# Attention scores in pairs of heads with one maximum and one exponential each, and a new table of beats for a four-layer kernel

## The chip, the cores and the metric

The kernel runs on one core of a Trainium2 chip. The metric is the time of one execution on the device, in microseconds (us); three runs of the kernel before gave 785.09, 787.24 and 787.25, median 787.24. The core has five engines that work side by side: TensorE (PE in the profile, with its weight loads as PEld), VectorE (DVE), ScalarE (ACT), GpSimd (POOL) and SyncE (SP, which here only issues transfers). They agree through semaphores alone.

## The reference

The input x has 8 images of 128 channels and 16 x 16 positions. Four layers follow each other; all arrays are float32.

```
x = gamma * (softmax(b @ c) @ d) + x        # L0: b, c (16 rows) and d (128 rows) are 1x1 convolutions of x
x = x + proj(attn(qkv(groupnorm(x))))       # L1: 8 heads of 16, all 256 positions of an image
t = tokens(x)                               # 256 tokens of 128 for each image
y = layernorm(t); t = t + softmax(y @ y.T) @ y                      # L2: self-attention without weights
y = layernorm(t); p = top-2 gate weights of softmax(y @ Wg)
t = t + sum over i in 0,1 and e in 0..7 of gelu((y * p_i) @ W1[e] + b1[e]) @ W2[e]    # d 128, dff 512, + b2
h = layernorm(t); q, k = rope(rmsnorm(h @ Wq)), rope(rmsnorm(h @ Wk))
t = t + softmax(q @ k.T / 4, keys s-31..s) @ v @ Wo                 # L3: 8 heads of 16, window of 32 tokens
h = layernorm(t); t = t + shared(h) + sum over the top 2 of 8 experts of p_e * (silu(h Wg_e) * (h Wu_e)) Wd_e
```

The dense experts of L2 run all 8 experts for both gate weights: 32 pieces of 128 hidden rows for each group of 512 tokens, 128 pieces in all.

## The kernel before, in words

**Tiling.** Work goes by groups of two images (512 tokens, 4 groups) and, in attention, by images. Attention is done sixteen times: images 0 to 7 in layer L1, then 8 to 15, which are the same images in layer L3. An attention is done in two halves of four heads each.

**Order.** Every engine runs the same outer loop over beats `s` (0 to LAST - 1, 224 of them) and issues, in a fixed order inside the beat, its share of whatever part stands in that beat. A beat is no length of time: a beat in which an engine has nothing to issue costs it nothing. Tables at lines 52 to 65 say in which beat a part stands: L0_AT (layer L0 of a group), P1_AT (norm and projection of L1), ATT_AT (an attention), TAIL_AT (output projection), L2_AT (self-attention and gates of L2), SPREAD_AT, FF_AT (first piece of the dense experts), END_AT, PREP_AT (norm, projection and rope of L3), ROUTER_AT and EXPERT_AT (the last mixture of experts). From beat FF_AT = 36 on, 128 beats hold one piece ("turn") of the dense experts each.

**One attention.** For image a, counted from its beat in ATT_AT: beats 0 and 2, scores of a half (`scores`, L399, queries in rows) and their row maxima on VectorE (`highest`, L1015); beats 1 and 3, the shifts so found are added to the queries' spare row (`add_shift`) after TensorE has turned them (`turn_shifts`, L413); beats 4 and 6, scores again with keys in rows (`scores_turned`, L431) and their exponentials on ScalarE (`exps`, L750, to ET); beats 5 and 7, the product with the values (`values`, L454); beat 8, the result is turned (`turn_o`, L467). In L1 two images stand four beats apart or less, so that parts of two halves alternate. In L3 a half's scores are 320 columns for a head in place of 512, and a product with a band constant puts the window's mask into the bank first (L391).

**Banks.** PSUM has 8 banks of 128 x 512. Bank 0 takes the up products of the dense experts, bank 2 their down products, banks 3 to 6 (QUAD_BANK) one half's scores, a bank for a head, and 1 and 7 (MISC) all else in turn. Each bank has a semaphore for filled and one for emptied; `take` waits until a bank is empty before TensorE writes. The last experts take gate, up and weight products into banks 0 and 3, 4 and 6, and 5.

**Dense experts.** A turn: up product into bank 0 (`ff_up`, two matmuls of 512 columns, L540), VectorE multiplies it by the two gate weights into z_s, 1024 wide (`ff_gate`, L1090, which empties the bank), ScalarE adds the bias and takes gelu (L809), GpSimd adds the two gated halves (`hidden`, L1278), TensorE multiplies down (`ff_down`, L547). Gelu and exponential need different function tables on ScalarE, so the gelus of eight turns are issued together.

**GpSimd** takes the normalisations between layers: `norm` first works out the roots (`newton`, L1264), then four products of 128 x 128 (L1271); also the group norm of L1 (L1258). Two sets of constants for the later layers are made in beats: `prepare_late` on GpSimd in beat 18, the rotary tables on VectorE (`tables`) in beat 34.

## Time and profile before

| what | value |
|---|---|
| median of three runs | 787.24 us |
| the profiled execution | 783.05 us |
| its span, from first to last instruction | 781.3 us |
| granted TensorE clock, mean over the span | 0.884 of full speed |
| TensorE busy | 633.1 us, 81% of the span |
| VectorE, ScalarE, GpSimd busy | 390.9, 343.4, 333.7 us |
| instructions | 9513 |
| chain that ended last | TensorE 51%, VectorE 16%, GpSimd 14%, issue 10%, ScalarE 8% |
| VectorE's gates (L1090) | 128, mean 1222 ns |
| row maxima (L1015) | 128, mean 583 ns |
| exponentials (L750) | 128, mean 522 ns, with 10 table loads of 1283 ns |

The profile is one execution recorded on the chip. "Busy" is the time in which an engine had an instruction under way. The chain that ended last is followed back from the last instruction, at each step to what released it, and its shares say on which engine the span was spent. The granted clock is the share of full speed that TensorE was allowed; it has two levels, 1.2 and 2.4 GHz, and a value between them is a mean over a stretch. A timeline lists instructions in order of their start; in brackets stands how long the engine had been idle before, and whose end released it.

### The profile page before, as it was taken

To read this page: it belongs to the slowest core of one execution; us is meant where nothing else is said; L and a number is where in the kernel's file an instruction comes from. 1 tells how busy PE (TensorE), PEld (TensorE's weight loads), DVE (VectorE), ACT (ScalarE), POOL (GpSimd) and SP (SyncE) were. 2 spreads that over 40 slices of the span, in tenths; PEclk is the share of its full clock that TensorE was granted. 3 is DMA by queue.
4 is the path that set the end of the run, shared out by engine and by line. 5 is a ranking of instruction groups with operands and counts; after the bars stand their busy time and mean duration, and the time that the engine had idled before them with its cause. 6 is when DMAs were issued, how large, how long until landed. Compare 5 with 4: busy or idle time off the path is not lost.

```text
span 781.3 us, 9513 instructions
## 1 busy us (share of the span) xinstructions
PE 633.1 (81%) x3266; PEld 324.7 (42%) x3266; DVE 390.9 (50%) x799; ACT 343.4 (44%) x544; POOL 333.7 (43%) x620
## 2 busy tenths in 40 slices
PE   7788988677888977887997869996689889757768
PEld 5565455444344442434443424442334344334422
DVE  3464441557375564674556385644675434531233
ACT  2423224136466465365455346653744634212222
POOL 2543411606174186696146685428671534200300
PEclk9997566789999999988999889999999999855789
DMA  6600000000000000000000000000000000000000
GB/s 211 146 1 1 1 1 1 0 1 1 1 0 1 1 1 1 1 0 0 2 0 2 0 1 0 1 1 1 0 0 1 1 1 14 13 1 1 0 14 13
DMA packets 10226, 8.59 MB, mean 11 GB/s; under 512 B 4026, under 2 KB 8132, under 8 KB 10180
## 3 DMA queue, kind: packets, MB, share of 16 engines
q1 hardware_dynamic: 10180, 8.00, 3.6%
q8 instruction: 27, 0.44, 0.3%
q14 instruction: 19, 0.16, 0.1%
HBM read 6.94 MB, written 1.05 MB: 10 GB/s over the span
## 4 chain that ended last, share of the span: by engine, by line
PE 51%; DVE 16%; POOL 14%; issue 10%; ACT 8%; DMA 0%; POOLq 0%; SPq 0%; DVEq 0%; ACTq 0%
PE bank L540 9%; PE bank L547 8%; POOL h_s L1278 4%; ACT ET L750 4%; DVE shiftpad L1015 4%; DVE z_s L1090 3%; POOL xn_l L1271 3%; PE bank L266 3%; PE bank L399 3%; PE bank L431 3%; PE bank L454 2%; PE bank L413 2%; PE bank L591 2%; PE bank L576 2%; PE bank L391 1%
## 5 line engine op out<-in xcount | busy, mean ns | idle before, releaser
L1090 DVE TENSOR_TENSOR z_s<-bank,PB 128x1024 f32<-128x1024 f32 x128 | 156.4, 1222 | 164.7 <-PE bank L540 162.6
L1278 POOL TENSOR_TENSOR h_s<-z_s 128x512 f32<-128x512 f32 x128 | 163.0, 1299 | 153.7 <-ACT z_s L809 135.4
L540 PE MATMUL bank<-XN_C,W 128*128 128x512 f32 x256 | 144.1, 646 | 34.3 <-DVE z_s L1090 33.7
L547 PE MATMUL bank<-h_s,W 128*128 128x512 f32 x256 | 145.3, 651 | 1.4 <-ACT y_s L816 1.0
L809 ACT ACTIVATE z_s<-z_s,b 128x1024 f32<-128x1024 f32 x128 | 137.2, 1141 | 11.0 <-DVE z_s L1090 10.8
L1015 DVE TENSOR_REDUCE shiftpad<-bank 128x2 f32<-128x512 f32 (+1 forms) x128 | 66.6, 583 | 53.9 <-PE bank L399 29.4
L540 PEld LDWEIGHTS bank<-XN_C,W 128*128 128x128 f32 x256 | 44.7, 199 | 101.8 <-DVE z_s L1090 79.3
L750 ACT ACTIVATE ET<-bank 128x512 f32<-128x512 f32 (+1 forms) x128 | 55.8, 522 | 57.0 <-PE bank L431 30.1
L1264 POOL TENSOR_SCALAR root_l<-mv_l 128x4 f32<-128x4 f32 x12 | 2.8, 232 | 168.8 <-DVE mv_l L1046 168.3
L547 PEld LDWEIGHTS bank<-h_s,W 128*128 128x128 f32 x256 | 44.5, 202 | 37.0 <-issue 31.4
L771 ACT COPY XN_C<-bank 128x512 f32<-128x512 f32 x16 | 9.4, 585 | 68.2 <-PE bank L266 68.1
L758 ACT COPY o_raw<-bank 128x256 f32<-128x256 f32 x32 | 11.9, 373 | 61.9 <-PE bank L454 37.5
L1271 POOL TENSOR_SCALAR xn_l<-R,mv_l,root_l 128x128 f32<-128x128 f32 x48 | 37.7, 800 | 1.3
L399 PE MATMUL bank<-K,Q 16*128 16x256 f32 x256 | 33.1, 514 | 3.8 <-ACT ET L750 3.8
L750 ACT ACT_TABLE_LOAD x10 | 12.8, 1283 | 51.8 <-PE bank L435 39.1
L1141 DVE TENSOR_TENSOR z_s<-z_s,bank 128x512 f32<-128x512 f32 (+1 forms) x20 | 13.7, 684 | 35.8 <-PE bank L579 27.6
L413 PE MATMUL bank<-ident,shiftpad 128*128 128x128 f32 x64 | 15.8, 336 | 18.6 <-DVE shiftpad L1015 17.0
L454 PE MATMUL bank<-ET,V 128*17 128x256 f32 x256 | 22.9, 488 | 7.3 <-ACT ET L750 5.2
L399 PEld LDWEIGHTS bank<-K,Q 16*128 16x128 f32 x256 | 21.7, 231 | 12.2 <-ACT ET L750 7.8
L266 PE MATMUL bank<-ident,xn_l 128*128 128x128 f32 x48 | 9.7, 336 | 18.4 <-POOL xn_l L1271 18.4
L413 PEld LDWEIGHTS bank<-ident,shiftpad 128*128 128x128 f32 x64 | 8.1, 166 | 38.7 <-issue 38.7
L840 ACT ACTIVATE z_s<-bank 128x512 f32<-128x512 f32 (+1 forms) x20 | 12.0, 602 | 25.8 <-PE bank L576 25.7
(246 smaller groups left out, 961.3 us busy)
## 6 DMA issues: line engine op xcount, KB each, us to landing
W<-in_L_ffn_W_dram SPq DMA_DIRECT2D x1, 2048.0 KB, 8.7
XN_C<-in_x_dram SPq DMA_DIRECT2D x4, 256.0 KB, 3.0
out_dram<-z_s SPq DMA_DIRECT2D x4, 256.0 KB, 2.2
Wgate<-in_L_ffn_W_gate_dram SPq DMA_DIRECT2D x1, 256.0 KB, 4.2
Wup<-in_L_ffn_W_up_dram SPq DMA_DIRECT2D x1, 256.0 KB, 4.8
Wdown<-in_L_ffn_W_down_dram SPq DMA_DIRECT2D x1, 256.0 KB, 4.3
early<-in_L_conv_W_qkv_dram SPq DMA_DIRECT2D x1, 192.0 KB
early<-in_L_conv_Wd_dram SPq DMA_DIRECT2D x1, 64.0 KB, 1.9
```

Of the source, the lines that this page charges most:

```text
L266: ins = nc.tensor.transpose(to[:, t * P:(t + 1) * P], source(t), ident[:, :])
L399: ins = nc.tensor.matmul(to[j][:, t * N:(t + 1) * N], q[:, t * P:(t + 1) * P], k, start=True, stop=True)
L413: ins = nc.tensor.transpose(to[:, t * P:(t + 1) * P], shiftpad[:, i % 2, t, :, :].rearrange("p j r -> p (j r)"), ident[:, :])
L454: ins = nc.tensor.matmul(to, v, E[:, kt * N:(kt + 1) * N], start=(kt == 0), stop=(kt == NT - 1), skip_group_check=True)
L540: nc.tensor.matmul(to[:, :], W1[:, f // 4, f % 4 * P:(f % 4 + 1) * P], XN_C[:, pair(g)], start=True, stop=True).then_inc(filled("u", t)[0], 1)
L547: ins = nc.tensor.matmul(bank[D_BANK][:, :], W2[:, f, :], h_s[:, t % H_RING, :], start=(f == 0), stop=(f == FT - 1)).then_inc(s_dn, 1)
L750: nc.scalar.activation(ET[:, i % 2 * SLOTS + j, 0:width(a)], content("T", (i, j))[:, 0:width(a)], ACT.Exp).then_inc(emptied("T", (i, j))[0 ...
L809: nc.scalar.activation(z, z, ACT.Gelu, bias=b1[:, f:f + 1]).then_inc(s_g, 1)
L1015: nc.vector.tensor_reduce(shiftpad[:, i % 2, :, j, HD], content("S", (i, j))[:, 0:width(a)].rearrange("p (t k) -> p t k", t=NT), AX.X, ALU ...
L1090: nc.vector.tensor_tensor(z_s[:, t % Z_RING, :].rearrange("p (w n) -> p w n", w=2), content("u", t)[:, None, :].broadcast_to([P, 2, W]), P ...
L1271: ins = nc.gpsimd.tensor_scalar(xn[n][:, c, :], R[:, tile(g, c)], mv[n][:, g, c, 0:1], y[:, c:c + 1], ALU.subtract, ALU.mult)
L1278: nc.gpsimd.tensor_tensor(h_s[:, t % H_RING, :], z_s[:, t % Z_RING, 0:W], z_s[:, t % Z_RING, W:2 * W], ALU.add).then_inc(s_h, 1)
```

## The change

Four things are changed together.

1. Banks 3 to 6 become one tensor `quad`. Scores and turned scores fill all four banks in their step and report each pair of heads with one semaphore (`KEEPER`, `fill`, `take_two`); `highest` and `exps` take two heads in one instruction (1024 columns in L1, 640 in L3). There are 64 of each in place of 128.
2. The steps of an attention are set by a table, `STEPS`. SLOW (images whose beat lies among the turns) puts shifts two beats behind scores, values two behind the turned scores, and the end in beat 9. FAST (images before the turns, and those behind beat 160) puts them in successive beats: scores 0 and 1, shifts and turned scores 1 and 2, values 2 and 3, end 4.
3. The beats are laid out anew. Turns begin at beat 32 and the last beat is 203. Layer L0 of groups 2 and 3 stands in beats 10 and 16, among the first attentions; all four projections of L1, layer L2 of group 0 and most of that of group 1 stand ahead of the first turn. The constants of `prepare_late` and `tables` move behind the first turn. In a beat, TensorE now issues shifts, values, turned scores and scores in this order.
4. The last experts take other banks: those of group 3 use banks 0 and 3, 1 and 5, and 7, the others bank 0 and the ring. Group 2's pass stands in the beats of the last attention, whose exponentials and sigmoid products use different tables on ScalarE.

The core of the diff:

```diff
-FF_AT = 36
+FF_AT = 32
 GELU_AT, DOWN_LAG = 5, 7
 Z_RING, H_RING = 8, 6
-L0_AT = (0, 3, 6, 9)
-P1_AT = (8, 12, 30, 44)
-ATT_AT = (9, 13, 17, 21, 33, 41, 49, 57, 89, 97, 121, 129, 153, 161, 185, 189)
-TAIL_AT = (22, 30, 50, 66, 106, 138, 170, 198)
-L2_AT = (27, 37, 61, 77)
-SPREAD_AT = (35, 45, 69, 101)
+L0_AT = (0, 3, 10, 16)
+P1_AT = (7, 13, 22, 28)
+ATT_AT = (8, 10, 14, 16, 37, 45, 53, 61, 93, 101, 117, 125, 149, 157, 179, 181)
+TAIL_AT = (15, 21, 56, 72, 112, 136, 168, 186)
+L2_AT = (20, 26, 61, 77)
+SPREAD_AT = (30, 40, 72, 104)
 END_AT = tuple(FF_AT + FT * (g + 1) + DOWN_LAG for g in range(GROUPS))
-PREP_AT = tuple(FF_AT + FT * g + 45 for g in range(3)) + (177,)
-ROUTER_AT = (113, 145, 177, 205)
-EXPERT_AT = (172, 178, 200, 211)
-LAST = 224
-
-U_BANK, D_BANK, QUAD_BANK, MISC = (0,), 2, 3, (1, 7)
-XG_BANK, XU_BANK, XW_BANK = (0, 3), (4, 6), 5
+PREP_AT = (81, 109, 141, 172)
+ROUTER_AT = (118, 141, 173, 191)
+EXPERT_AT = (168, 174, 180, 196)
+LAST = 203
+U_BANK, D_BANK, QUAD_BANK, MISC, MISC_FIRST = 0, 2, 3, (1, 7), (1, 7, 0)
+KEEPER = (0, 1, 2, 3, 3, 5, 5, 7)
+SLOW = {"S": (0, 2), "MT": (2, 4), "T": (4, 6), "PV": (6, 8), "OT": 9, "later": 0}
+FAST = {"S": (0, 1), "MT": (1, 2), "T": (1, 2), "PV": (2, 3), "OT": 4, "later": 0}
+STEPS = [FAST if at < FF_AT or at > FF_AT + TURNS else SLOW for at in ATT_AT]
...
+            def fill(what, i, banks):
+                kept = KEEPER[banks[0]]
+                was = max(content_of[b] for b in banks)
+                if was:
+                    pe.wait_ge(bank_emptied[kept], was)
+                fills[kept] += 1
+                for b in banks:
+                    content_of[b] = fills[kept]
+                turn_of[what, i] = banks[0], fills[kept]
+                return bank[banks[0]]
             def take(what, i, b=None):
-
                 if b is None:
-                    b = MISC[turns[0] % len(MISC)]
-                    turns[0] += 1
-                if fills[b]:
-                    pe.wait_ge(bank_emptied[b], fills[b])
-                fills[b] += 1
-                turn_of[what, i] = b, fills[b]
-                return bank[b]
+                    ring = MISC if beat[0] >= FF_AT else MISC_FIRST
+                    turns[ring] += 1
+                    b = ring[turns[ring] % len(ring)]
+                return fill(what, i, (b,))
+            def take_two(what, i, jj):
+                return fill(what, i, (QUAD_BANK + 2 * jj, QUAD_BANK + 2 * jj + 1))
...
-                to = [take("S", (i, j), QUAD_BANK + j) for j in range(SLOTS)] if a >= IMAGES else [None] * SLOTS
+                for jj in range(2):
+                    take_two("S", (i, jj), jj)
...
-                        if t == NT - 1:
-                            ins.then_inc(filled("S", (i, j))[0], 1)
+                        if t == NT - 1 and j % 2 == 1:
+                            ins.then_inc(filled("S", (i, j // 2))[0], 1)
...
-            def exps(a, half):
+            def exps(a, half, jj):
                 i = a * 2 + half
-                if i >= 2:
+                if i >= 2 and jj == 0:
                     act.wait_ge(*filled("pv", i - 2))
-                for j in range(SLOTS):
-                    act.wait_ge(*filled("T", (i, j)))
-                    nc.scalar.activation(ET[:, i % 2 * SLOTS + j, 0:width(a)], content("T", (i, j))[:, 0:width(a)], ACT.Exp).then_inc(
-                        emptied("T", (i, j))[0], 1)
+                at = i % 2 * SLOTS + 2 * jj
+                act.wait_ge(*filled("T", (i, jj)))
+                nc.scalar.activation(ET[:, at:at + 2, 0:width(a)], quad[:, 2 * jj:2 * jj + 2, 0:width(a)], ACT.Exp).then_inc(emptied("T", (i, jj))[0], 1)
...
-            def highest(a, half):
+            def highest(a, half, jj):
                 i = a * 2 + half
-                if i >= 2:
-                    dve.wait_ge(*filled("MT", i - 2))
-                elif i == 0:
-                    dve.wait_ge(s_pads, 5)
-                for j in range(SLOTS):
-                    dve.wait_ge(*filled("S", (i, j)))
-                    nc.vector.tensor_reduce(shiftpad[:, i % 2, :, j, HD], content("S", (i, j))[:, 0:width(a)].rearrange("p (t k) -> p t k", t=NT),
-                                            AX.X, ALU.max, negate=True).then_inc(emptied("S", (i, j))[0], 1)
+                if jj == 0:
+                    if i >= 2:
+                        dve.wait_ge(*filled("MT", i - 2))
+                    elif i == 0:
+                        dve.wait_ge(s_pads, 5)
+                at = slice(2 * jj, 2 * jj + 2)
+                dve.wait_ge(*filled("S", (i, jj)))
+                nc.vector.tensor_reduce(shiftpad[:, i % 2, :, at, HD].rearrange("p t j -> p j t"),
+                                        quad[:, at, 0:width(a)].rearrange("p j (t k) -> p j t k", t=NT),
+                                        AX.X, ALU.max, negate=True).then_inc(emptied("S", (i, jj))[0], 1)
...
-                    to = take("xg", (g, k), XG_BANK[k % 2])
+                    to = take("xg", (g, k), (0, QUAD_BANK)[k % 2 if g == GROUPS - 1 else 0])
...
-                    to = take("xu", (g, k), XU_BANK[k % 2])
+                    to = take("xu", (g, k), (1, 5)[k % 2] if g == GROUPS - 1 else None)
...
-                        to = take("xw", (g, k), XW_BANK)
+                        to = take("xw", (g, k), 7 if g == GROUPS - 1 else None)
...
-                if s == 34:
+                if s == FF_AT:
...
-                if s == 18:
+                if s == FF_AT + 10:
```

Loops that named beats by `k in (0, 2)` and the like now compare with STEPS in the same way on all engines; lines below L262 move down by some 20 to 28.

What stands in TensorE's row one step before the turns, in the attention of images 2 and 3: before,

```order
L399 MATMUL bank<-K,Q 128x256 x8
L454 MATMUL bank<-ET,V 17x256 x8
L413 MATMUL bank<-ident,shiftpad 128x128 x2
L431 MATMUL bank<-Q,K 128x256 x8
L399 MATMUL bank<-K,Q 128x256 x8
L454 MATMUL bank<-ET,V 17x256 x8
L413 MATMUL bank<-ident,shiftpad 128x128 x2
L467 MATMUL bank<-ident,o_raw 128x128 x4
L431 MATMUL bank<-Q,K 128x256 x8
L399 MATMUL bank<-K,Q 128x256 x8
```

and now:

```order
L420 MATMUL quad<-K,Q 128x256 x8
L320 MATMUL bank<-XN_C,Wbc 128x512
L287 MATMUL bank<-ident,XN_C 128x128 x4
L326 MATMUL bank<-WdT,XN_C 128x128 x4
L434 MATMUL bank<-ident,shiftpad 128x128 x2
L475 MATMUL bank<-ET,V 17x256 x8
L452 MATMUL quad<-Q,K 128x256 x8
L502 MATMUL bank<-Wp,oT 128x128 x4
L420 MATMUL quad<-K,Q 128x256 x8
```

L399 (now L420) are scores, L431 (L452) turned scores, L454 (L475) values, L413 (L434) shifts, L467 and L502 parts of the output. Before, one kind of product follows another of the other half and the values stand two rows behind the scores; now layer L0 of another group stands between scores and shifts, and values and turned scores follow the shifts directly.

In TensorE's row ahead of the first up product (L540, now L561): before,

```order
L481 MATMUL bank<-Wp,oT 128x128 x4
L266 MATMUL bank<-ident,xn_l 128x128 x4
L399 MATMUL bank<-K,Q 128x256 x8
L527 MATMUL bank<-Wg,XN_C 128x8 x4
L266 MATMUL bank<-ident,xn_l 128x128 x4
L413 MATMUL bank<-ident,shiftpad 128x128 x2
L399 MATMUL bank<-K,Q 128x256 x8
L266 MATMUL bank<-ident,gate 128x128 x8
L540 MATMUL bank<-XN_C,W 128x512
```

and now:

```order
L537 MATMUL bank<-xn_l,early 128x128 x8
L287 MATMUL bank<-ident,xn_l 128x128 x8
L548 MATMUL bank<-Wg,XN_C 128x8 x4
L518 MATMUL bank<-XN_C 128x256 x4
L527 MATMUL bank<-ident,early 128x128 x8
L376 MATMUL quad<-XN_C,Wqk 128x512 x4
L379 MATMUL bank<-WvT,XN_C 128x128 x4
L537 MATMUL bank<-xn_l,early 128x128 x8
L287 MATMUL bank<-ident,gate 128x128 x8
L287 MATMUL bank<-ident,xn_l 128x128 x4
L561 MATMUL bank<-XN_C,W 128x512
```

Here L266 (L287) turns a normalised or gate tile, L527 and L548 `Wg` are gate logits, L516 (L537) with `early` is the self-attention of L2, L376 and L379 a projection of L1. The projection of group 3 and all of group 1's layer L2 up to the turning of its normalised tokens (`xn_l` x4) now stand ahead of the first up product, where scores of two images stood.

In ScalarE's row at the last attention (ET is the exponential, o_raw a copy of the values' product): before,

```order
L750 ACT_TABLE_LOAD
L750 ACTIVATE ET<-bank 128x320 x4
L758 COPY o_raw<-bank 128x256
L750 ACTIVATE ET<-bank 128x320 x4
L758 COPY o_raw<-bank 128x256
L750 ACTIVATE ET<-bank 128x320 x4
L758 COPY o_raw<-bank 128x256
L750 ACTIVATE ET<-bank 128x320 x4
L758 COPY o_raw<-bank 128x256
```

and now:

```order
L776 ACT_TABLE_LOAD
L776 ACTIVATE ET<-quad 128x2x320 x2
L865 ACT_TABLE_LOAD
L865 ACTIVATE z_s<-bank 128x512
L783 COPY o_raw<-bank 128x256
L776 ACT_TABLE_LOAD
L776 ACTIVATE ET<-quad 128x2x320 x2
L865 ACT_TABLE_LOAD
L865 ACTIVATE z_s<-bank 128x512
L783 COPY o_raw<-bank 128x256
```

The activation of an expert block (z_s, L865) now stands between the exponentials of two halves, and a table load ahead of each; ACT has 42 table loads in all, 36 before.

## Rows read from the trace of the kernel before

**Rows 1.** Windows: us, busy (instructions) of each engine, PEclk, DMA share, GB/s.

```profile
66.00:131.00 65.00, 56.47 (x370) 33.73 (x370) 23.25 (x52) 20.98 (x45) 20.27 (x57) 0.61 0.00 1
78.30:89.30 11.00, 10.01 (x71) 4.82 (x70) 5.77 (x11) 2.44 (x5) 8.79 (x22) 0.66 0.00 0
161.60:612.00 450.40, 374.66 (x1859) 177.88 (x1858) 261.94 (x441) 247.20 (x346) 243.64 (x373) 0.95 0.00 1
682.80:731.00 48.20, 31.49 (x253) 19.63 (x254) 9.80 (x24) 9.06 (x22) 0.00 (x0) 0.50 0.00 1
```

**Rows 2.** Timeline to the first up product: start, us, instruction, idle before and releaser.

```profile
138.78 0.24 POOL L1264 TENSOR_SCALAR root_l<-mv_l 128x4 f32<-128x4 f32 x1 [17.89 <-DVE mv_l L1046]
...
142.79 3.14 POOL L1271 TENSOR_SCALAR xn_l<-R,mv_l,root_l 128x128 f32<-128x128 f32 x4
...
161.64 1.91 PE L540 MATMUL bank<-XN_C,W 128*128 128x512 f32 x2
```

**Rows 3.** Timeline of VectorE: gates.

```profile
163.69 1.23 DVE L1090 TENSOR_TENSOR z_s<-bank,PB 128x1024 f32<-128x1024 f32 x1 [3.87 <-PE bank L540]
...
228.50 1.21 DVE L1090 TENSOR_TENSOR z_s<-bank,PB 128x1024 f32<-128x1024 f32 x1
...
302.69 1.23 DVE L1090 TENSOR_TENSOR z_s<-bank,PB 128x1024 f32<-128x1024 f32 x1 [1.29 <-PE bank L540]
...
483.12 1.22 DVE L1090 TENSOR_TENSOR z_s<-bank,PB 128x1024 f32<-128x1024 f32 x1 [0.25 <-PE bank L540]
...
507.62 1.22 DVE L1090 TENSOR_TENSOR z_s<-bank,PB 128x1024 f32<-128x1024 f32 x1 [0.28 <-PE bank L540]
...
612.26 1.23 DVE L1090 TENSOR_TENSOR z_s<-bank,PB 128x1024 f32<-128x1024 f32 x1 [0.96 <-PE bank L540]
```

**Rows 4.** Timeline of one step of the attention before the experts.

```profile
83.27 2.06 ACT L750 ACTIVATE ET<-bank 128x512 f32<-128x512 f32 x4 [2.27 <-PE bank L431]
84.01 3.45 PE L399 MATMUL bank<-K,Q 16*128 16x256 f32 x16 [0.82 <-ACT ET L750]
...
86.73 2.48 DVE L1015 TENSOR_REDUCE shiftpad<-bank 128x2 f32<-128x512 f32 x4 [3.86 <-PE bank L399]
87.39 1.91 PE L454 MATMUL bank<-ET,V 128*17 128x256 f32 x16
...
90.06 2.09 PE L431 MATMUL bank<-Q,K 17*128 17x256 f32 x16
...
92.88 3.53 PE L399 MATMUL bank<-K,Q 16*128 16x256 f32 x16 [0.73 <-ACT ET L750]
```

**Rows 5.** Timeline: first projection and scores, and the last values before the experts.

```profile
28.62 2.45 POOL L1258 TENSOR_SCALAR XN_C<-XN_C,gm,root 128x256 f32<-128x256 f32 x2
...
36.69 3.60 PE L355 MATMUL bank<-XN_C,Wqk 128*128 128x512 f32 x8
...
45.76 1.15 PE L399 MATMUL bank<-K,Q 16*128 16x256 f32 x16
...
131.17 1.06 PE L454 MATMUL bank<-ET,V 128*17 128x256 f32 x16 [0.81 <-ACT early L783]
```

**Rows 6.** Timeline of TensorE behind the dense experts.

```profile
672.62 1.97 PE L576 MATMUL bank<-XN_C,Sgate 128*64 128x512 f32 x2
...
676.99 1.91 PE L266 MATMUL bank<-ident,early 128*128 128x128 f32 x16
...
682.87 1.23 PE L391 MATMUL bank<-bandb,identb 128*128 128x320 bf16 x4 [2.92 <-ACT K L742]
...
751.17 1.06 PE L561 MATMUL bank<-router,XN_C 128*128 128x8 f32 x8
```

**Rows 7.** Timeline of ScalarE: table load and exponentials of the last attention.

```profile
695.84 1.28 ACT L750 ACT_TABLE_LOAD   x1 [13.31 <-PE bank L435]
697.14 1.43 ACT L750 ACTIVATE ET<-bank 128x320 f32<-128x320 f32 x4
```

More of the change, by code:

```diff
@@ L441, in values @@
                 i = a * 2 + half
-                for j in range(SLOTS):
-                    pe.wait_ge(*emptied("T", (i, j)))
+                for jj in range(2):
+                    pe.wait_ge(*emptied("T", (i, jj)))
                 if half == 0:
@@ L598, in _ @@
             for s in range(LAST):
+                beat[0] = s
                 for g in range(GROUPS):
@@ L618, in _ @@
                 for a in range(2 * IMAGES):
-                    k = s - ATT_AT[a]
-                    if k in (0, 2):
-                        scores(a, k // 2)
-                    if k in (1, 3):
-                        turn_shifts(a, k // 2)
+                    for half in range(2):
+                        if s == ATT_AT[a] + STEPS[a]["S"][half]:
+                            scores(a, half)
                 if 0 <= s - FF_AT - DOWN_LAG < TURNS:
```

99 lines of the change are left out of this document (54 added, 45 removed).

## The prediction

> **What bounds the kernel now.** I read the windows by stage first. In the long middle stage, the 128 turns of the dense experts, TensorE is busy 374.66 of 450.4 us at a clock of 0.95, and no other engine passes 262 [rows 1]. In the attention of the last two images, 48.2 us, TensorE is busy 31.49 us and the clock is 0.50, the lower of its two levels (1.2 of 2.4 GHz). In the attention before the experts, 66 to 131 us, it is 0.61, although TensorE is busy 56.47 of 65. So there are three stages with three limits: a chain of dependent steps at a low clock, a stage nearly full of matmuls, and a chain again. The first up product stands at 161.64 [rows 2], which makes stage A; its gates run from 163.69 to 612.26 [rows 3], stage B; the rest to 781.3 is C.
>
> Second, the timeline of one step of A. From scores to scores it is 92.88 - 84.01 = 8.87 us [rows 4]; TensorE idles only 0.73 to 0.82 in it, on the exponentials. The maxima (2.48) and exponentials (2.06) of one half lie beside the products of another image's half. Scores or turned scores take 2.09 at the low level; at the high one 1.15 [rows 5].
>
> Third, the gates of B. Alone, a turn lasts 1.29 + 1.23 = 2.52 us: gate, next up product into the one bank, gate. An image of layer 3 with its eight beats takes 507.62 - 483.12 = 24.50 [rows 3], not far above 8 x 2.52 = 20.2.
>
> **Merged instructions.** Two heads' maxima are now one instruction of 1024 columns. VectorE's gate of 1024 took 1.23 [rows 3], four maxima of 512 take 2.48 [rows 4], so two wide ones cost 2.46 by the gate, at best 2.2 if half of the fixed part falls away, at worst 2.5. ScalarE's four exponentials take 2.06; two wide ones I bound by 1.9 and 2.3 in the same way and take 2.1. The merge itself is worth nothing I can see; what it changes is grain. Scores now wait for both exponentials before their first product, where before the banks came free one at a time.
>
> **Stage A.** (1) The start gets earlier. Group 0 is normalised on POOL at 28.62 + 2.45 = 31.07, yet its projection stood at 36.69, behind products of group 2 [rows 5]. Now it follows group 1 directly: 31.1 + 3.6 for the projection + 1.2 for what stands between = scores at 35.9, against 45.76. (2) The steps get longer. Before the experts, transposed shifts, turned scores, and the scores of the next half stand in one beat, so a half's whole path lies in line: maximum 2.0 to 2.1 behind the scores, shifts 0.4 (0.7 at the low level), values of the half before 1.0 (1.91), which hide the addition of the shift, turned scores 1.15 (2.09), exponentials less the part beside the products 1.75 (1.6), scores 1.15 (2.09). That is 7.5 at the high level and 10.4 at the low. Seven steps are 53 or 73. The last half's rest to its values adds 9.3 or 12. Group 1's projection and the parts of groups 2 and 3 that stick out of the waits add 9 or 12. The eighth values end at 35.9 + 71.3 = 107 or 133; before, 131.17 + 1.06 = 132.2 [rows 5]. (3) More stands between them and the first up product: two groups' layer 2, two projections. POOL normalises three things in a row, and one such took 138.78 to 145.93, 7.15 [rows 2]. From the eighth values: 5 until POOL has its first, 3 x 7.15 for three, 13 for gate logits, scores, turning, projection and output of group 1's layer 2, then 10.5 for its statistics (2.5), POOL again (7.15) and its turning, which stands ahead of the first up product in TensorE's row: 50, and 58 at the low level. Before, it was 29.4. First up product: 157 or 191. With nearly half of the way at each level I take 174: A = +12, between -4 and +29.
>
> At this place a row and a rule meet. The row: the clock was 0.50 where TensorE waited a third of the time, but 0.61 also where it waited little [rows 1]. The Trainium skill (TensorE: Matmul & The Clock Gate, "A second HAM failure mode: psum-queue depth-cycling") says that a TensorE which idles briefly between groups of matmuls while banks go round swings between its two levels and loses throughput. The trace agrees, and shows the low level with little idling too. By that rule alone A would be +29; by the full level it would be -4.
>
> **Stage B.** Before, 448.6 us. The first sixteen turns took 228.50 - 163.69 = 64.8 [rows 3], since group 1's layer 2, group 3's projection and an image stood in them. Those two now lie in A. What is left: five turns alone, 5 x 2.52 = 12.6; three beats with scores, where a gate stands behind two wide maxima, 3.5 each, 10.5; eight beats of an image of layer 1, at 3.15 each a little above the 24.50 / 8 = 3.06 of layer 3, 25.2: 48.3, so -16.5. Images of layer 3: the beats with two kinds of products get longer (values 0.6 into the beat of turned scores), the emptied ones fall no lower than 2.52; 24.5 +- 1 against 24.50, nothing. The stalls on maxima and exponentials in the other images of layer 1 go, by my estimate 1.5 each for three: -4.5. What is late next there is the gate. Other tails, routers and projections trade collisions on POOL, 0 +- 6. B = -21, between -6 and -28. POOL's late constants, 22 instructions over 11.0 us [rows 1], move into the tenth turn; POOL's idle half of B covers them, and without that cover they cost up to 11. The rotary tables move to turn 0 and hold one gate for about 1 us, which I leave in the rounding.
>
> **Stage C.** The turning of the last queries (676.99) stood behind the fourth block of an expert pass, which begins at 672.62 [rows 6]; it is now before it, but ScalarE takes that block's activation ahead of the copies. Scores start 5.9 us after the turning now, 6.1 then: -4. Ahead of that, POOL does the experts' norm before the attention's and TensorE waits less for maxima and exponentials: -4, bounds 0 and -11. Then four steps in line, with the third group's expert blocks in them, which before followed until the router at 751.17, 68.3 after the first scores. Each step has two switches of ScalarE's table. In line: gate product 1.0, load 1.3, activation 0.6, two products on VectorE 1.4, shift 0.4, turned scores 1.6, load 1.3, two exponentials of 640 columns 1.4, scores 1.7, and 0.4 of signals: 11.1. First scores to second 11, three steps and the rest of the fourth 29, then values, last blocks, output projection and norm 24.5: 64.5 at the high level, some 13 more at the low one. In between, 71: +3. The last pass is as long as before. C = -5, between -12 and +2.
>
> The row on loads: the load starts at 695.84, the first exponential at 697.14, so 1.30 each [rows 7]. The Trainium skill (ScalarE: Activation LUTs, "Table sets: the hidden batching unit") advises against this change: do all calls of one table set together; and its section "What ACT_TABLE_LOAD costs" gives some 2.66 us a switch with draining. The trace shows no such drain. By the page the six more switches would cost an estimated 8 us more and the sum below would rise by that.
>
> **Sum.** 783.05 + 12 - 21 - 5 = 769 for the profiled execution (span 781.3 and 1.75 around it). The median of the runs, 787.24, is 4.2 above that execution; carried over, 773.
>
> **Rivals.** First, slower: the clock stays low through both chains. Place: the half's path in line in A and C; price: 17 us in A and 7 in C on top of the forecast, that is A +29, B -21, C +2, 793, with the 4.2 797. For it: 0.50 and 0.61 [rows 1]. Against: layer 0 and expert products of 128 rows now stand in the steps. It decides from the point where about four fifths of both chains are at the low level: A + C run from -16 to +31, and at +21 the gain of B is eaten. Second, the high level nearly throughout: A -4, C -12, B -21: 746, so 750. For it the same products; against it the waits of 2 us in each step. Third, the change doesn't do in B what it says: the gate's round trip of 2.52 fills every emptied beat, and the first sixteen turns save only 10 and the layer 3 images cost 1 each for four: B = -6, sum 784, so 788, no change or a little slower. For it [rows 3]; against it only that the moved products surely leave.
>
> **Chances.** Forecast 0.48, low clock 0.20, high clock 0.20, beats bound 0.12. The forecast's own range is 760 to 786. The range to 8 in 10 goes from 749 to 798, which takes in the ends of A and C. About 0.3%, 2.4 us, is what a measurement tells from no change. Faster: 0.48 less 0.02, 0.20, and 0.05 of the third, 0.71. Same: 0.02 and 0.04, 0.06. Slower: the first and the rest of the third, 0.23.
>
> **What would show it.** First scores near 36 and eighth values between 107 and 133, with the clock of that stretch beside; the first up product between 157 and 191, waiting for POOL's norm; sixteen turns in about 48; an image of layer 3 in 24 to 25.5; wide maxima of 1.2 and wide exponentials near 1.05; a step of the last attention near 11 with loads of 1.3. I am wrong if the first up product comes before 150, if an image of layer 3 falls under 23, or if a wide instruction takes twice the time of two narrow ones.

## The result, and the profile after

The changed kernel takes 806.28 us (median of four runs, 805.22 to 807.16) beside 786.32 for the kernel before: ratio 1.0254, 95% interval 1.0231 to 1.0277, slower. 773 was forecast, with 798 as the upper end. The profiled execution took 805.89, its span is 804.0; that is 22.7 more than before.

Cut at the gates into the prediction's stages, with the stage of the turns in two, from the timelines of VectorE (A ends with the first gate):

| kernel | A | first 16 turns | other turns | C | span |
|---|---|---|---|---|---|
| before | 163.7 | 64.8 | 383.8 | 169.0 | 781.3 |
| changed | 182.1 | 56.9 | 397.8 | 167.3 | 804.0 |
| difference | +18.4 | -7.9 | +14.0 | -1.7 | +22.7 |
| forecast | +12 | -16.5 | -4.5 | -5 | -14 |

The gates that make the cuts, from VectorE's timeline of the changed kernel (start, us, instruction, idle before); they answer to [rows 3]:

```profile
182.12 1.22 DVE L1118 TENSOR_TENSOR z_s<-bank,PB 128x1024 f32<-128x1024 f32 x1 [11.31 <-PE bank L561]
...
188.90 1.23 DVE L1118 TENSOR_TENSOR z_s<-bank,PB 128x1024 f32<-128x1024 f32 x1 [2.17 <-PE bank L561]
192.30 1.22 DVE L1118 TENSOR_TENSOR z_s<-bank,PB 128x1024 f32<-128x1024 f32 x1 [1.68 <-PE bank L561]
...
238.98 1.21 DVE L1118 TENSOR_TENSOR z_s<-bank,PB 128x1024 f32<-128x1024 f32 x1
...
636.73 1.22 DVE L1118 TENSOR_TENSOR z_s<-bank,PB 128x1024 f32<-128x1024 f32 x1 [0.67 <-PE bank L561]
```

A turn alone takes 192.30 - 188.90 = 3.40 here; in [rows 3] it took 2.52. The windows say why (us, busy and instructions of each engine, granted clock, DMA share, GB/s), as in [rows 1]:

```profile
36.20:126.00 89.80, 68.87 (x539) 43.92 (x540) 37.53 (x71) 27.91 (x49) 18.31 (x55) 0.75 0.00 1
126.00:179.90 53.90, 30.52 (x150) 22.82 (x150) 17.03 (x63) 13.92 (x34) 24.59 (x73) 0.78 0.00 0
179.90:213.00 33.10, 26.15 (x63) 10.64 (x64) 16.85 (x34) 8.32 (x8) 7.53 (x6) 0.50 0.00 0
182.10:636.70 454.60, 375.00 (x1836) 179.50 (x1837) 256.56 (x406) 237.74 (x293) 244.30 (x375) 0.92 0.00 1
```

The first row is the attention of images 0 to 3, the second what stands between its last values and the first up product: there TensorE is busy 30.5 of 53.9 us. The third row is the first turns, at 0.50, the low level.

TensorE's timeline of stage A, which answers to [rows 2] and [rows 5]:

```profile
36.22 1.15 PE L420 MATMUL quad<-K,Q 16*128 16x256 f32 x16
...
124.94 1.06 PE L475 MATMUL bank<-ET,V 128*17 128x256 f32 x16 [0.16 <-issue]
...
145.37 0.88 PE L287 MATMUL bank<-ident,xn_l 128*128 128x128 f32 x4 [3.40 <-POOL xn_l L1301]
152.56 1.11 PE L287 MATMUL bank<-ident,xn_l 128*128 128x128 f32 x4 [6.31 <-POOL xn_l L1301]
...
178.06 1.11 PE L287 MATMUL bank<-ident,xn_l 128*128 128x128 f32 x4 [8.85 <-POOL xn_l L1301]
179.94 2.05 PE L561 MATMUL bank<-XN_C,W 128*128 128x512 f32 x2 [0.77 <-ACT XN_C L796]
```

The eighth values end at 126.0, 6.2 earlier than before. From there to the first up product it is 53.9 us in place of 29.4, and 18.6 of them are three waits for GpSimd's norms.

Among the other turns the two longest are turn 108, 11.1 us from gate to gate, and turn 44, 10.0. GpSimd and TensorE around turn 44:

```profile
327.43 0.23 POOL L1294 TENSOR_SCALAR root_ff<-mv_ff 128x4 f32<-128x4 f32 x1 [1.02 <-DVE mv_ff L1074]
...
337.07 0.23 POOL L1294 TENSOR_SCALAR root_l<-mv_l 128x4 f32<-128x4 f32 x1
...
341.04 3.13 POOL L1301 TENSOR_SCALAR xn_l<-R,mv_l,root_l 128x128 f32<-128x128 f32 x4
```

```profile
336.80 1.12 PE L561 MATMUL bank<-XN_C,W 128*128 128x512 f32 x2
344.23 1.11 PE L287 MATMUL bank<-ident,xn_l 128*128 128x128 f32 x4 [6.30 <-POOL xn_l L1301]
345.14 1.92 PE L568 MATMUL bank<-h_s,W 128*128 128x512 f32 x2
```

The end of a group's experts (beat 71) and group 3's output projection (beat 72) each need a norm on GpSimd; they run one after the other, and TensorE stands in its row at the second one's turning (L287) for 6.3 us with every later turn behind it. Turn 108 is the same pair (beats 135 and 136), with a wait of 6.56:

```profile
570.44 1.11 PE L287 MATMUL bank<-ident,xn_l 128*128 128x128 f32 x4 [6.56 <-POOL xn_l L1301]
```

### The profile page after: what moved, and what is told of

Its sections match the earlier page's. It is cut to its first block, busy times and chain, and to the rows that moved or that the text cites. A ratio compares the mean times of both kernels' runs of the same rounds, so it can differ in the third digit from the quotient of the medians.

```text
span 804.0 us, 9310 instructions
## 1 busy us (share of the span) xinstructions
PE 631.7 (79%) x3266; PEld 325.0 (40%) x3266; DVE 383.5 (48%) x735; ACT 346.9 (43%) x486; POOL 333.1 (41%) x620
## 4 chain that ended last, share of the span: by engine, by line
PE 50%; DVE 17%; POOL 14%; issue 11%; ACT 6%; DMA 0%; POOLq 0%; DVEq 0%; SPq 0%; ACTq 0%
PE bank L561 10%; DVE z_s L1118 7%; PE bank L568 7%; POOL h_s L1308 5%; POOL xn_l L1301 3%; PE bank L597 3%; PE quad L420 2%; DVE shiftpad L1042 2%; PE quad L452 2%; ACT ET L776 2%; PE bank L287 2%; PE bank L612 2%; PE bank L475 2%; PE quad L376 2%; PE bank L600 1%
## 5 line engine op out<-in xcount | busy, mean ns | idle before, releaser
L561 PE MATMUL bank<-XN_C,W 128*128 128x512 f32 x256 | 151.0, 674 | 47.9 <-DVE z_s L1118 46.4
L568 PE MATMUL bank<-h_s,W 128*128 128x512 f32 x256 | 143.0, 644 | 7.3 <-POOL h_s L1308 7.3
L561 PEld LDWEIGHTS bank<-XN_C,W 128*128 128x128 f32 x256 | 46.1, 207 | 126.5 <-DVE z_s L1118 103.3
L1042 DVE TENSOR_REDUCE shiftpad<-quad 128x4 f32<-128x1024 f32 (+1 forms) x64 | 62.5, 1019 | 62.6 <-PE quad L420 33.9
L776 ACT ACTIVATE ET<-quad 128x1024 f32<-128x1024 f32 (+1 forms) x64 | 51.8, 861 | 30.3 <-PE quad L452 24.4
L568 PEld LDWEIGHTS bank<-h_s,W 128*128 128x128 f32 x256 | 45.2, 199 | 47.9 <-issue 33.9
L783 ACT COPY o_raw<-bank 128x256 f32<-128x256 f32 x32 | 11.9, 372 | 86.3 <-PE bank L479 43.7
L287 PE MATMUL bank<-ident,xn_l 128*128 128x128 f32 x48 | 10.8, 365 | 45.1 <-POOL xn_l L1301 45.1
L420 PE MATMUL quad<-K,Q 16*128 16x256 f32 x256 | 22.3, 470 | 11.0 <-ACT ET L776 10.8
L1277 POOL TENSOR_TENSOR R<-early,bp_all 128x512 f32<-128x512 f32 x4 | 5.1, 1267 | 61.3 <-DVE early L974 61.3
L287 PEld LDWEIGHTS bank<-ident,xn_l 128*128 128x128 f32 x48 | 6.9, 180 | 51.4 <-POOL xn_l L1301 50.9
L865 ACT ACTIVATE z_s<-bank 128x512 f32<-128x512 f32 (+1 forms) x18 | 10.7, 596 | 29.1 <-PE bank L597 29.1
L434 PE MATMUL bank<-ident,shiftpad 128*128 128x128 f32 x64 | 14.7, 317 | 10.9 <-issue 8.5
L452 PE MATMUL quad<-Q,K 17*128 17x256 f32 x256 | 21.2, 452 | 1.1 <-DVE Q L1050 1.0
```

Of the source, the lines that this page charges most:

```text
L287: ins = nc.tensor.transpose(to[:, t * P:(t + 1) * P], source(t), ident[:, :])
L420: ins = nc.tensor.matmul(to[:, t * N:(t + 1) * N], q[:, t * P:(t + 1) * P], k, start=True, stop=True)
L452: ins = nc.tensor.matmul(to[:, t * N:(t + 1) * N], k[:, t * P:(t + 1) * P], q, start=True, stop=True)
L561: nc.tensor.matmul(to[:, :], W1[:, f // 4, f % 4 * P:(f % 4 + 1) * P], XN_C[:, pair(g)], start=True, stop=True).then_inc(filled("u", t)[0], 1)
L568: ins = nc.tensor.matmul(bank[D_BANK][:, :], W2[:, f, :], h_s[:, t % H_RING, :], start=(f == 0), stop=(f == FT - 1)).then_inc(s_dn, 1)
L776: nc.scalar.activation(ET[:, at:at + 2, 0:width(a)], quad[:, 2 * jj:2 * jj + 2, 0:width(a)], ACT.Exp).then_inc(emptied("T", (i, jj))[0], 1)
```

## The experiments

Ratios are to the kernel before, run beside them on the same chip, with 95% intervals. Stages, in us, are those of the one profiled execution. For e3, e8 and e10 it took 7.8, 6.6 and 4.2 us more than the median of the runs; for the others it lies within 2.7 of it.

| kernel | A | first 16 | other turns | C | span |
|---|---|---|---|---|---|
| e1 | 186.9 | 57.0 | 398.2 | 164.8 | 806.9 |
| e2 | 183.1 | 69.4 | 379.0 | 165.2 | 796.7 |
| e5 | 163.9 | 70.1 | 379.8 | 160.4 | 774.2 |
| e6 | 182.5 | 55.9 | 398.2 | 162.7 | 799.3 |
| e4 | 162.7 | 58.5 | 399.8 | 164.0 | 785.0 |
| e8 | 183.7 | 57.3 | 404.6 | 164.6 | 810.2 |
| e11 | 183.9 | 55.2 | 400.6 | 165.9 | 805.6 |
| e3 | 182.0 | 56.8 | 405.7 | 165.4 | 809.9 |
| e10 | 181.9 | 56.8 | 387.9 | 164.8 | 791.4 |
| e12 | 162.2 | 58.5 | 389.7 | 164.8 | 775.2 |
| e13 | 167.8 | 70.2 | 382.5 | 161.2 | 781.8 |
| e7 | 168.6 | 65.9 | 377.5 | 166.0 | 778.1 |
| e9 | 159.2 | 60.6 | 404.2 | 162.9 | 786.9 |

**1. e1_unmerged: the merge undone alone.**

```diff
-KEEPER = (0, 1, 2, 3, 3, 5, 5, 7)
+KEEPER = tuple(range(8))
...
-                nc.scalar.activation(ET[:, at:at + 2, 0:width(a)], quad[:, 2 * jj:2 * jj + 2, 0:width(a)], ACT.Exp).then_inc(emptied("T", (i, jj))[0], 1)
+                for j in (2 * jj, 2 * jj + 1):
+                    act.wait_ge(*filled("T", (i, j)))
+                    nc.scalar.activation(ET[:, i % 2 * SLOTS + j, 0:width(a)], quad[:, j, 0:width(a)], ACT.Exp).then_inc(emptied("T", (i, j))[0], 1)
```

> Changed kernel with only the merge undone: one bank, one semaphore and one maximum or exponential for each head again, all tables and the order in a beat as changed. Theory 1 (the loss is in the tables: work moved ahead of the first up product, and GpSimd norms that now meet; the merge is worth nothing): 806 us, at most 3 away, ratio to before 1.021 to 1.030. Rival theory 2 (the wide instructions cost: scores wait for both exponentials, a gate waits behind a wide maximum): under 800, ratio under 1.018. In both four narrow maxima take about 2.4 to 2.5, as before.

807.38, ratio 1.028 (1.0245 to 1.0315), beside 1.0254 (1.0231 to 1.0277) with the merge: it neither costs nor gives anything clear of the noise. The forms of the changed kernel say the same (busy us, mean ns | idle before):

```profile
L1042 DVE TENSOR_REDUCE shiftpad<-quad 128x4 f32<-128x1024 f32 x32 | 37.7, 1220 | 33.9 <-PE quad L420 33.9
L776 ACT ACTIVATE ET<-quad 128x1024 f32<-128x1024 f32 x32 | 31.0, 1021 | 24.5 <-PE quad L452 24.4
```

Before, the same work in 64 instructions of 512 columns each was busy 39.6 and 33.0:

```profile
L1015 DVE TENSOR_REDUCE shiftpad<-bank 128x2 f32<-128x512 f32 x64 | 39.6, 682 | 29.4 <-PE bank L399 29.4
L750 ACT ACTIVATE ET<-bank 128x512 f32<-128x512 f32 x64 | 33.0, 602 | 30.1 <-PE bank L431 30.1
```

**2. e2_old_tables: the new code with the tables of before.**

```diff
-FF_AT = 32
+FF_AT = 36
...
+STEPS = [{"S": (0, 2), "MT": (1, 3), "T": (4, 6), "PV": (5, 7), "OT": 8, "later": 0} for at in ATT_AT]
```

> Changed kernel with all tables of before, the step offsets of before, and the late constants in the beats of before; wide instructions, paired banks, expert banks and the order inside a beat stay as changed. Theory 1 (tables): as before, 783 to 790, ratio 0.996 to 1.004; first gate near 164, gates over 448 us. Rival theory 2 (code: wide instructions, or shifts and values ahead of turned scores in a beat, cost): over 795, ratio above 1.012.

796.97, ratio 1.0145 (1.0104 to 1.0187). That is the rival's time: A is 183.1 against 163.7, while the other turns gain, 379.0 against 383.8. The code has a cost of its own in A; e1 says that it isn't the merge. A step of A in the timelines of TensorE and VectorE:

```profile
91.92 2.09 PE L420 MATMUL quad<-K,Q 16*128 16x256 f32 x16 [2.18 <-ACT ET L776]
94.10 2.36 DVE L1042 TENSOR_REDUCE shiftpad<-quad 128x4 f32<-128x1024 f32 x2 [4.68 <-PE quad L420]
96.56 0.66 PE L434 MATMUL bank<-ident,shiftpad 128*128 128x128 f32 x2 [2.55 <-issue]
97.15 1.91 PE L475 MATMUL bank<-ET,V 128*17 128x256 f32 x16
98.99 2.09 PE L452 MATMUL quad<-Q,K 17*128 17x256 f32 x16
103.25 2.09 PE L420 MATMUL quad<-K,Q 16*128 16x256 f32 x16 [2.17 <-ACT ET L776]
```

11.3 us against the 8.87 of [rows 4]. The shifts' turning (L434) now stands ahead of the values (L475), and TensorE stands still 2.55 us while VectorE takes the maxima, which end at 96.46 ("issue" means that the profile names no releaser); before, the values stood in that gap. The 2.17 ahead of the scores is no loss: before, the scores began after 0.73 and stretched to 3.53, the same 4.26 in sum.

**3. e5_old_tables_values_first: e2 with values ahead of shifts again.** The loop over "PV" and "OT" is put ahead of the loop over "MT" in TensorE's beat.

> The kernel with changed code and the tables of before (e2), with one swap: in a beat TensorE issues the values' product and the turning of the output ahead of the shifts' turning, as before the change. Theory 1 (the order in the beat cost e2 its 19.4 us in stage A: with shifts first, TensorE waits out the wide maxima, 2.55 us in each of eight steps, and nothing covers them): first gate from 183 back to 163 to 168, time 777 to 783. Rival theory 2 (scores that wait for both wide exponentials, 2.1 us in each step, cost it): first gate stays above 176, time above 790.

778.4, ratio 0.9922 (0.989 to 0.9954), faster than before. A is back at 163.9; the wait fell to 0.71:

```profile
84.31 2.09 PE L420 MATMUL quad<-K,Q 16*128 16x256 f32 x16 [2.18 <-ACT ET L776]
86.33 1.91 PE L475 MATMUL bank<-ET,V 128*17 128x256 f32 x16
88.95 0.66 PE L434 MATMUL bank<-ident,shiftpad 128*128 128x128 f32 x2 [0.71 <-issue]
```

One swap of two products moved a stage by 19.1 us. What e5 gains over the kernel before stands in C (160.4 against 169.0); which part of the changed code gives it was not tested.

**4. e6_values_first: the same swap in the changed kernel, ahead of the first turn only.**

> Changed kernel with the same swap, in the beats ahead of the first turn alone. Theory 1: the maxima are then covered by the values, but the addition of the shift no longer is: each of eight steps saves 0.5 to 1, first gate 174 to 178, time 798 to 802. Rival theory (layer 0 of groups 2 and 3 covers the maxima already, what bounds stage A is the work behind the eighth values): within 2 us of 806.

802.44, ratio 1.0208 (1.0133 to 1.0284); A 182.5, as it was. In these tables the order doesn't decide A; which products cover the maxima here was not followed. The interval takes in the changed kernel's 1.0254, so the 4 us are not clear of the noise; they are in C (162.7), which the edit doesn't touch, and over the nine kernels with these tables C ranges from 162.7 to 167.3.

**5. e4_work_back: layer 2 of group 1 and the projection of group 3 among the first turns again.**

```diff
-P1_AT = (7, 13, 22, 28)
+P1_AT = (7, 13, 22, 40)
-L2_AT = (20, 26, 61, 77)
-SPREAD_AT = (30, 40, 72, 104)
+L2_AT = (20, 33, 61, 77)
+SPREAD_AT = (30, 42, 72, 104)
```

> Changed kernel with layer 2 of group 1 (beat 33) and the projection of group 3 (beat 40) back among the first turns, as they stood before. Theory 1 (in front of the first turn this work runs alone, with TensorE waiting on GpSimd's norm and at the low clock; among the turns it is partly hidden): first gate from 182 to 158 to 165, first sixteen turns from 57 to 66 to 70, sum 793 to 799. Rival theory (it costs the same at either place, as the prediction took it, 16.5 us): first gate falls by 16 and the turns grow by 16, within 3 us of 806.

786.71, ratio 1.0023 (0.9988 to 1.0057). A falls by 19.4 to 162.7, and the first sixteen turns, which take all that work back, grow by 1.6 to 58.5. Windows of this kernel (columns as above):

```profile
162.00:186.00 24.00, 18.68 (x67) 9.66 (x67) 15.69 (x37) 7.88 (x15) 8.38 (x20) 0.75 0.00 0
186.00:222.00 36.00, 33.05 (x193) 16.16 (x191) 23.95 (x32) 23.63 (x27) 23.64 (x34) 1.00 0.00 1
```

With the work in them the turns fill TensorE, and the clock is at the high level from 186 on. So the 1.6 is a net figure: it holds what the work adds less what the clock gives back, 3.39 - 2.52 for each lone turn, and the two were not measured apart.

**6. e8_keep_busy: idle products in the waits of A.**

```diff
+            def keep_busy(to, n):
+                for _ in range(n):
+                    nc.tensor.matmul(to[:, 0:P], ident[:, :], ident[:, :], start=True, stop=True)
...
+                    keep_busy(to, 8)
                 for jj in range(2):
                     pe.wait_ge(*emptied("S", (i, jj)))
```

> Changed kernel with idle products added ahead of the first turn: 8 of 128 x 128 ahead of each wait for the maxima and for the exponentials, 24 ahead of each wait for a normalisation; nothing else changed. Theory 1 (the waits let the clock fall to the low level, which stretches every product of stage A by up to 1.8 and carries into the first turns): granted clock between 36 and 180 us from 0.77 to over 0.9, first gate 165 to 175, first sixteen turns from 57 to 50 to 53, time 785 to 797. Rival theory (the chain is set by VectorE, ScalarE and GpSimd, and added products only come on top): first gate 182 or later, time 804 or more.

805.28, ratio 1.0232 (1.0174 to 1.029); A 183.7. The granted clock of A rose to 0.98, and A stayed as long:

```profile
36.00:180.00 144.00, 127.76 (x1120) 103.53 (x1119) 54.37 (x131) 40.83 (x82) 42.37 (x124) 0.98 0.00 1
```

This does not show that the low clock costs A nothing. From the first scores to the first up product (at 181.53) the kernel's own products keep TensorE busy 74.9 us, where they took 99.4 in the changed kernel, and its idle time falls from 44 to 17; but the added products take 53.6. They stand in its row also where the changed kernel had no wait, as behind the eighth values (the first line is of the changed kernel, the others are of this one):

```profile
125.93 0.66 PE L287 MATMUL bank<-ident,xn_l 128*128 128x128 f32 x4
...
124.83 5.62 PE L435 MATMUL bank<-ident 128*128 128x128 f32 x48
130.29 0.60 PE L529 MATMUL bank<-ident,xn_l 128*128 128x128 f32 x4
```

What the clock gave, the added products took again. How long A would be at the high level without them stays open.

**7. e11_busy_at_first_turn: 52 idle products in the one wait ahead of the first turn.** The edit is that of e8, in the turning of group 1's layer 2 alone.

> Changed kernel with 52 idle products of 128 x 128 in the one wait of 8.9 us ahead of the first up product, so that TensorE comes to the first turn without having idled. Theory 1 (that wait lets the clock fall to the low level, at which it stays until some 213 us, and a turn alone takes 3.39 in place of 2.51 there): first gate 180 to 184 as it was, the first five turns 2.5 to 2.6 each, first sixteen turns 57 to 50 to 52, time 799 to 802. Rival theory (the clock falls for want of work in the turns themselves): first sixteen turns stay at 56 to 58, time within 3 us of 806.

806.85, ratio 1.026 (1.0196 to 1.0324); first sixteen turns 55.2. My theory fell:

```profile
180.00:192.00 12.00, 7.62 (x34) 4.11 (x32) 6.08 (x24) 5.41 (x6) 2.87 (x3) 0.92 0.00 0
192.00:213.00 21.00, 16.73 (x48) 6.44 (x48) 11.07 (x10) 3.44 (x3) 4.68 (x4) 0.50 0.00 1
```

TensorE came to the first turn at the high level and lost it in the emptied turns themselves, where it is busy with one up product between gates.

**8. e3_pool_apart: the two projections some beats later, so that GpSimd's norms no longer meet.**

```diff
-TAIL_AT = (15, 21, 56, 72, 112, 136, 168, 186)
+TAIL_AT = (15, 21, 56, 76, 112, 142, 168, 186)
-L2_AT = (20, 26, 61, 77)
+L2_AT = (20, 26, 61, 81)
-PREP_AT = (81, 109, 141, 172)
-ROUTER_AT = (118, 141, 173, 191)
+PREP_AT = (85, 109, 141, 172)
+ROUTER_AT = (118, 147, 173, 191)
```

> Changed kernel with the output projection of group 3 in layer 1 four beats later (76) and that of group 1 in layer 3 six later (142), and what hangs on them (layer 2 of group 3 at 81, group 0's layer 3 preparation at 85, group 1's router at 147). Then no normalisation on GpSimd stands directly behind that of the dense experts. Theory 1 (two norms of 7.2 us back to back made turns 44 and 108 take 10.0 and 11.1): these turns fall to 2.5 to 5, 12 to 16 us in all, of which some comes back where the later norms meet other GpSimd work: 790 to 798. Rival theory (the wait only moves to the next product that needs the same engine): within 3 us of 806.

803.81, ratio 1.0257 (1.0207 to 1.0308): nothing. Turns 40 to 48 fell from 36.0 to 20.6, and turns 48 to 64 rose from 47.9 to 65.9. The wait moved to later turnings, that of the same norm at turn 48 and that of the next preparation of layer 3 at turn 59:

```profile
350.22 1.11 PE L287 MATMUL bank<-ident,xn_l 128*128 128x128 f32 x4 [2.49 <-POOL xn_l L1301]
...
395.41 3.68 PE L287 MATMUL quad<-ident,early 128*128 128x128 f32 x16 [4.11 <-DVE early L1029]
...
592.63 1.11 PE L287 MATMUL bank<-ident,xn_l 128*128 128x128 f32 x4 [5.98 <-POOL xn_l L1301]
```

The last line is what became of the 6.56 at turn 108.

**9. e10_later_turn: the projections' norms on GpSimd where they were, TensorE's turning of them two beats later.** ScalarE's copy of the turned tiles, layer 2 of groups 2 and 3 and the router of group 1 follow two beats later too; these lines are left out here.

```diff
-                elif k == 4:
+                elif k == (6 if ap >= 2 and ap < 6 else 4):
                     norm_turn("l1" if ap < GROUPS else "l3", ap % GROUPS)
```

> Changed kernel in which TensorE turns a normalised output projection six beats behind its start in place of four, in the four that stand among the turns; what must follow moves (layer 2 of groups 2 and 3 to 63 and 79, group 1's router to 143). GpSimd's work stands where it stood. Theory 1 (GpSimd has its two norms of 7.2 us back to back, but TensorE stands in its row only two beats behind: it is TensorE's place that costs turns 44 and 108 their 10.0 and 11.1): these two turns fall to 3 to 6, time 794 to 800. Rival theory (as in e3, what is not waited for here is waited for at the next product that needs GpSimd): within 3 us of 806.

788.99, ratio 1.0049 (1.002 to 1.0078). The other turns fall by 9.9 to 387.9, but not at turn 44. The 6.30 there are 3.16 with two more turns done ahead of it, and layer 2's norm, which had no wait, now has 4.51:

```profile
345.50 0.66 PE L287 MATMUL bank<-ident,xn_l 128*128 128x128 f32 x4 [3.16 <-POOL xn_l L1301]
...
374.24 1.11 PE L287 MATMUL bank<-ident,xn_l 128*128 128x128 f32 x4 [4.51 <-POOL xn_l L1301]
...
566.32 0.66 PE L287 MATMUL bank<-ident,xn_l 128*128 128x128 f32 x4
```

Turns 16 to 64 take 171.0, 172.2 in the changed kernel: there the wait passed on, as the rival has it. Turns 64 to 127 take 216.8 for 225.5. The last line is the turning that waited 6.56 at turn 108 and now waits for nothing; some of it comes back at turn 114. There it is TensorE's place in its row that cost, with GpSimd's norms where they were.

**10. e12_back_and_later: e4 and e10 in one.**

> e4 and e10 in one: changed kernel with layer 2 of group 1 and the projection of group 3 back among the first turns, and TensorE turning the normalised projections two beats later. Theory 1 (the two causes are separate, one ahead of the first turn and one among the turns, so their gains add: 19.4 us and 10 to 13): time 771 to 777, ratio 0.983 to 0.991. Rival theory (work put back among the turns takes the room that e10 gained there, as e9's pieces did not add): 780 or more.

776.65, ratio 0.9905 (0.9872 to 0.9938): by stages the two causes are separate. A -19.9, first turns +1.6, other turns -8.1 against the changed kernel. By the ratios, e4 and e10 take 2.3% and 2.1% off the changed kernel's and both together 3.5%, so about 7 us of the sum are missing, a little more than the intervals allow, and no stage shows where. With this version the changed layout beats the kernel before.

**11. e13_old_tables_later: e5 with the later turning.**

> e5 (changed code, tables of before, values ahead of shifts) with the later turning of e10 and no other table moved. The tables of before also have a projection and the end of a group's experts in neighbouring beats (turns 74 and 106 took 5.9 and 6.5 in e5). Theory 1 (TensorE's place in its row costs there too): these turns fall below 4, time 770 to 776 beside e5's 778. Rival theory (in that order GpSimd does the projection's norm first and the wait only passes to the experts' norm two rows on): within 2 us of e5.

780.89, ratio 0.9979 (0.9942 to 1.0017): no gain over e5. In the tables of before the projection stands a beat ahead of the experts' end, and the wait passes to the latter, as the rival has it: at turn 75 it is 2.60 in e5 (first line) and 6.00 here, and at turn 107 6.00 again, while the projection's own turning no longer waits.

```profile
439.87 0.66 PE L287 MATMUL bank<-ident,xn_ff 128*128 128x128 f32 x4 [2.60 <-POOL xn_ff L1301]
...
443.75 1.11 PE L287 MATMUL bank<-ident,xn_ff 128*128 128x128 f32 x4 [6.00 <-POOL xn_ff L1301]
```

The eight turns around each pair rose from 32.9 and 33.8 to 35.5 and 35.2.

**12. Two joinings that did not add up.** e7_front_new_rest_old took the front of e4 and, among the turns, the beats of before; e9_joined packed the images of layer 1 at 36, 43, 50, 57 on top, took the end of before, and had values ahead of shifts throughout.

> Changed code; ahead of the first turn the tables of e4 (layer 2 of group 1 and the projection of group 3 among the first turns), from the first turn on the beats and step offsets of before, moved by the four beats that the turns begin earlier; the last attention and the last experts as changed. Theory 1 (stages add: A 163 to 168 of e4, first sixteen turns 58 to 64, the rest of the turns 379 of e2, the end 164 to 166): 766 to 778. Rival theory (the old offsets lose among the turns what the new front gains): 783 or more.

> Joined from the stages measured so far, code as changed: ahead of the first turn the tables of e4; among the turns the images of layer 1 at 36, 43, 50, 57, then the beats and step offsets of before moved by four; the end as before the change; values ahead of shifts everywhere as in e5. If stages add: A 163 of e4, first sixteen turns 59 to 64, turns 16 to 64 164, the rest of the turns 212, the end 161 to 165 (e5, e2): span 759 to 768, time 761 to 770, ratio to before 0.970 to 0.981. If the sum up to turn 64 is the same whatever stands where (397 to 400 in four kernels so far): time 773 to 778, ratio 0.984 to 0.991.

782.09, ratio 0.9955 (0.9926 to 0.9984), and 790.08, ratio 1.0059 (1.0032 to 1.0086). In e7, A (168.6) and the first turns (65.9) came out above the sum. In e9, A was 159.2 and the first turns 60.6, but turns 16 to 32 took 74.5, 52.8 to 61.4 in the others. That seven beats for an image are too few is my reading; it was not tested alone. Neither of its two expectations held, nor either of e7's.

## Why the prediction was wrong

**Right: the merge.** Two wide maxima take 2.36 to 2.44, forecast 2.46; two wide exponentials 2.04, forecast 2.1; undoing them changes nothing clear of the noise (e1).

**Right: the working of A, at +18.4 within its -4 to +29.** First scores at 36.22 (35.9 forecast), eighth values at 126.0 (107 to 133), from them to the first up product 53.9 (50 to 58). It named the wait too: GpSimd's norms in a row behind the eighth values.

**Where the miss lies.** The span was to fall by 14 and rose by 22.7. Of the 36.7 us between, 18.5 stand in the other turns, 8.6 in the first sixteen, 6.4 in A and 3.2 in C. Stage B failed, in both of its terms.

**The step that failed, first term: "What is left: ... 48.3, so -16.5."** The first sixteen turns took 56.9: the five lone turns 17.0 for 12.6, the eight beats of the image 29.3 for 25.2, the three beats with scores 10.6 for 10.5. What remains was priced at the high clock, and up to 213 us it stood at 0.50: a lone turn, put at 2.52, took 3.39, and e11 shows that the emptied turns themselves lose the level. The gain was also put down to the two parts that leave. e4 measured them: put back, they cost a net 1.6 among the turns, with the clock's rise in it, and 19.4 ahead of them. [rows 3] could have told, as I read it now: a lone turn is 1.29 and 1.23, up product and gate in turn, so TensorE has nothing to do beside the gate; what stood in those turns stood in that gap, and the gap stays when it goes. My A and B were added as if apart; they exchanged work at a bad rate.

**The second and larger term: "Other tails, routers and projections trade collisions on POOL, 0 +- 6" and the -4.5.** The other turns grew by 14.0 in place of falling by 4.5. Most of it is in turns 64 to 127: 225.5, for 214.0 before. The new beats do it: the five kernels with the order of before there (e2, e5, e7, e9, e13) take 212.5 to 216.4. Turns 44 and 108 alone stand 16 over two lone turns; the corresponding turns of before (74, 75, 106, 107) stood 12 over four. The order of beats 71 and 72, 135 and 136 stands in the tables, and two norms of 7.15 us [rows 2] against two turns of 2.52 could have been worked out. e10 took 8.7 back in these turns. Turns 16 to 64 took 172.2 for 169.8, with one image of layer 1 more in them (that of beat 61; before, the first of the four began ahead of the turns), for which the sum had nothing. Whether the three stalls went as forecast can't be told apart from that.

**Images of layer 3** nearly kept their length: five of them took 23.9 to 26.5 over eight turns, 24.0 to 24.8 before, forecast 24.5 +- 1. The emptied beats stand at 2.51, as the gate's round trip said.

**C: -1.7, forecast -5, within its range.** Ahead of the first scores it lost 8.4 (forecast 8), and from there to the router (L582) it takes 74.4, forecast 71, 68.3 before. A step takes 14.6 and 13.5 us; 11.1 was its price at the high clock, and from 706 to 740 the granted clock was 0.60:

```profile
698.90 0.70 PE L413 MATMUL quad<-bandb,identb 128*128 128x320 bf16 x4 [1.05 <-ACT K L768]
...
708.59 1.23 PE L413 MATMUL quad<-bandb,identb 128*128 128x320 bf16 x4 [2.81 <-ACT ET L776]
...
723.19 1.22 PE L413 MATMUL quad<-bandb,identb 128*128 128x320 bf16 x4 [2.81 <-ACT ET L776]
...
736.66 1.23 PE L413 MATMUL quad<-bandb,identb 128*128 128x320 bf16 x4 [2.82 <-ACT ET L776]
...
773.28 1.87 PE L582 MATMUL bank<-router,XN_C 128*128 128x8 f32 x8 [0.67 <-ACT XN_C L796]
```

**The rivals.** The low clock through both chains gave 797 and lay nearest, but by luck: it asked for the low level over four fifths of both chains and left B's gain whole. The mean clock was 0.76 from 36 to 180 us and 0.67 from 704 to 758, which by the two levels is half and two thirds of the time at the low one, and it is B's gain that was missing. What the low clock costs in A alone no run here shows (e8). The rule of the Trainium skill weighed there (TensorE: Matmul & The Clock Gate, "A second HAM failure mode: psum-queue depth-cycling") agrees with the swings of the clock in these rows (means of 0.75 and 0.78, between the two levels); that ending them buys time, no run here shows. The third rival, that B does not fall, was right in direction: it put B at -6, and it was +6.0.

**Not foreseen at all:** values behind shifts. In the changed tables it costs nothing that e6 shows, in those of before 19 us (e2, e5), where nothing else covers VectorE's maxima. The prediction saw that values then "hide the addition of the shift", and not what they had hidden before.

**Open:** what the low clock costs in A, what e4's work adds among the turns at one and the same clock, and why C moves by 4.6 us between kernels whose C is the same.

## What to carry to other kernels

Price work that is moved twice: what it adds where it goes, and what the place it leaves really becomes without it; a stage full of matmuls gives back far less than the work's own time when the work stood in its gaps. Of an engine that issues in order, count not only how long the helper takes, but how far behind the helper's start the waiting product stands. Two beats later was worth 8.7 us here in the turns of layer 3, and nothing in those where layer 2 follows directly; moving the helper's work apart gave nothing. When two neighbouring products in a row are swapped, ask of each which wait it covered.
